# Attention over 32-row blocks in an attention and expert kernel on one core: probabilities turned by VectorE, x of two batches normalised by GpSimd

## What is computed

```python
h = layernorm(x)                                  # no weights
q, k, v = h @ Wq + bq, h @ Wk + bk, h @ Wv + bv
probs = softmax(q @ k.T / sqrt(128))              # per batch, 512 x 512, no mask
x = x + layernorm(probs @ v)
h = layernorm(x)
spikes = sigmoid(h @ W_enc + b_enc)               # 256
cont = spikes @ W_s2c + b_s2c                     # 64
gate = top 2 of softmax(cont @ Wr + br) of 8 experts, made to sum to 1
out = sum_e gate[e] * (relu(cont @ W1[e] + b1[e]) @ W2[e] + b2[e])
dec = sigmoid(out @ W_c2s + b_c2s) @ W_dec + b_dec
x = x + layernorm(layernorm(dec) * ln_g + ln_b)
```

## Time and profile before

| what | value |
|---|---|
| median of 3 runs | 131.04 us (131.02 to 132.98) |
| profiled execution | 130.91 us, its span 129.0 us |
| granted TensorE clock in it, mean | 0.995 |
| TensorE busy | 118.7 us, 92% of the span |
| TensorE weight loads | 80.1 us, beside matmuls |
| VectorE | 94.4 us, 73% |
| ScalarE | 58.8 us, 46% |
| GpSimd | 33.8 us, 26% |
| DMA | 12.42 MB, mean 96 GB/s |

### The profile page before, as it was taken

The page is one execution under the profiler, slowest core; times in us unless marked ns, Lnnn a source line. Parts: engine busy times, 40 slices in busy tenths (PEclk is TensorE's granted clock), DMA queues, the critical chain, the costliest instruction groups (busy, mean ns, idle before and its releaser), DMA issues.

```text
span 129.0 us, 2501 instructions
## 1 busy us (share of the span) xinstructions
PE 118.7 (92%) x815; PEld 80.1 (62%) x815; DVE 94.4 (73%) x400; ACT 58.8 (46%) x173; POOL 33.8 (26%) x70
## 2 busy tenths in 40 slices
PE   6999999999999989999999999999998899998920
PEld 2556786878645767754575994657565455864910
DVE  0858537698989874788957168966889999389672
ACT  1647765556837575204666542053713003903620
POOL 4423503325231162220000132230081043330551
PEclk9999999999999999999999999999999999999998
DMA  3558800000000019700000198000019749720022
GB/s 113 132 121 227 234 18 3 0 0 3 0 5 0 0 50 324 290 8 0 0 0 0 41 293 329 3 0 0 8 48 319 299 138 323 276 86 0 4 79 81
DMA packets 9370, 12.42 MB, mean 96 GB/s; under 512 B 3169, under 2 KB 5998, under 8 KB 9358
## 3 DMA queue, kind: packets, MB, share of 16 engines
q1 hardware_dynamic: 8254, 12.08, 28.5%
q10 hardware_dynamic: 1104, 0.20, 0.8%
HBM read 11.16 MB, written 1.11 MB: 95 GB/s over the span
## 4 chain that ended last, share of the span: by engine, by line
PE 54%; DVE 23%; issue 8%; POOL 7%; ACT 3%; DMA 2%; POOLq 1%; DVEq 0%
PE ps_t L942 10%; POOL rstd L431 7%; PE ps_s L804 6%; PE ps_o L829 6%; PE ps_s L918 5%; PE ps_c L918 4%; DVE stats L1172 3%; PE ps_o L858 3%; PE ps_t L816 3%; DVE x_out L1366 2%; DMA x_in<-in_L_attn_x 2%; DVE xn L1184 2%; PE ps_o L918 2%; PE ps_a L769 2%; DVE neg_max L1200 2%
## 5 line engine op out<-in xcount | busy, mean ns | idle before, releaser
L431 POOL TENSOR_TENSOR rstd<-var_eps,minus_half 128x2 f32<-128x2 f32 (+1 forms) x33 | 25.4, 771 | 88.9 <-DVE var_eps L1177 47.3
L829 PEld LDWEIGHTS ps_o<-v,probsT 128*128 128x128 f32 x128 | 15.6, 191 | 4.6 <-ACT probsT L546 4.1
L829 PE MATMUL ps_o<-v,probsT 128*128 128x128 f32 x128 | 17.5, 279 | 0.4 <-ACT probsT L546 0.3
L942 PE MATMUL ps_t<-gated,w 128*64 128x256 f32 x128 | 17.0, 389 | 0.9 <-DVE gated L1286 0.8
L804 PE MATMUL ps_s<-xnT,yT 128*128 128x512 f32 x32 | 16.0, 596 | 0.1
L541 ACT ACTIVATE probs<-ps_s,neg_max 128x512 f32<-128x512 f32 x16 | 11.0, 687 | 11.1 <-DVE neg_max L1200 11.0
L1200 DVE TENSOR_REDUCE neg_max<-ps_s 128x1 f32<-128x512 f32 x16 | 10.9, 689 | 5.0 <-PE ps_s L804 4.9
L942 PEld LDWEIGHTS ps_t<-gated,w 128*64 128x64 f32 x128 | 8.0, 136 | 8.8 <-DVE gated L1286 4.2
L1286 DVE SCALAR_TENSOR_TENSOR gated<-ps_s,b_minus,gate_all 128x512 f32<-128x512 f32 x14 | 9.9, 744 | 1.9 <-PE ps_s L918 1.9
L546 ACT ACTIVATE probsT<-ps_t 128x512 f32<-128x512 f32 x16 | 9.5, 594 | 2.6 <-PE ps_t L816 2.4
L562 ACT ACTIVATE spikes<-ps_o,bias_half 128x512 f32<-128x512 f32 x6 | 4.1, 687 | 13.5 <-PE ps_o L858 13.4
(11 more groups left out here) (207 smaller groups left out, 218.6 us busy)
## 6 DMA issues: line engine op xcount, KB each, us to landing
gate_all<-gates SPq DMA_DIRECT2D x12, 512.0 KB, 6.0
gate_all<-gates SPq DMA_DIRECT2D x8, 256.0 KB, 3.6
x_in<-in_L_attn_x SPq DMA_DIRECT2D x3, 256.0 KB, 3.6
w<-in_L_ffn_W SPq DMA_DIRECT2D x3, 256.0 KB, 4.4
out<-x_out SPq DMA_DIRECT2D x3, 256.0 KB, 2.0
x_in<-in_L_attn_x SPq DMA_DIRECT2D x2, 128.0 KB, 2.5
out<-x_out SPq DMA_DIRECT2D x2, 128.0 KB, 1.7
w_enc<-in_L_ffn_W_enc SPq DMA_DIRECT2D x1, 128.0 KB, 2.7
```

What stands on the lines that cost most here:

```text
L431: nc.gpsimd.tensor_tensor(rstd[part], var_eps[part], minus_half[:, t0:t1], ALU.pow).then_inc(g_rstd[n], 1)
L829: mm = nc.tensor.matmul(attn_out(t), probsT[:, b % 2, t, k], v[:, b % 2, k], start=(k == 0), stop=(k == T - 1))
L942: mm = nc.tensor.matmul(ps_t[h * M:(h + 1) * M, 0:SH], w2[:, e], gated[:, e, h * SH:(h + 1) * SH], start=False, stop=(e == E - 1))
```

## The change

Batch 0 is done as before. For batches 1 to 3:

- VectorE turns each 128x512 tile of probabilities in 32x32 blocks (`turn_blocks`, one instruction per tile, twelve in all), in place of four TensorE transposes and a ScalarE copy. In `blocks` a partition then holds a key of its 32-key group, and four row groups i of 32 partitions hold four groups of queries.
- `attend(b)` is one step of 64 matmuls: each takes 32 rows (keys), 128 queries as weights and 129 columns of v; the four row groups write to four banks, `ps_o[:, i]`. Column 129 of v is ones, so the product brings the sum of the probabilities, and `exps` doesn't sum any more. For the queries of a row group to be 128 that lie together, `y_out` writes yT in another order of columns.
- Every row group needs all keys' v: v goes to DRAM and returns as v_all, 4 transfers of 32 partitions, 1 MB per batch, on SP's queue ahead of the gates.
- ScalarE copies the product (`att_out`, 128x516), and squares and x_mid read the copy.
- x of batches 2 and 3 is normalised by GpSimd (`x_norm`, L478), and the statistics of x_mid in these two batches are replaced by ScalarE's squares (`mid_square`) against the mean of x, with a small `mid_var` on VectorE.
- Batch 0's last norm goes to ScalarE and GpSimd (`z_norm`, `z_add`), where batch 1's was already. The output is written over x_in, and some other buffers are shared.
- ps_c is gone and ps_o has four banks, in pairs PAIR_X and PAIR_Y; ps_s is PAIR_S. The lists of all engines are written anew; the folding of the biases comes after `attend(1)`, `decode` is one step, and `attend(3)` waits for all eight gate products of batch 0.

The diff, cut to the buffers, the new steps and the parts of the lists of which something is said:

```diff
...
         probs = sb("probs", [P, 2, T, S])
-        probsT = sb("probsT", [P, 2, T, T, P])
+        blocks = sb("blocks", [P, 2, S // 32, T, 32])
+        v_all = sb("v_all", [P, 2, T, T, D + 1])
+        probsT = blocks[:, 0].rearrange("p (t a) b r -> p t a (b r)", t=T)
+        att = sb("att", [P, 2, T, D + 1])
         squares = sb("squares", [P, 2, T, D])
...
+        PAIR_S, PAIR_X, PAIR_Y = ps_s, ps_o[:, 0:2], ps_o[:, 2:4]
...
+        def attn_sums(b, t0, t1):
+            return prob_sum[:, t0:t1] if b == 0 else att[:, b % 2, t0:t1, D]
...
+            sp.wait_ge(g_v_ones, 1)
+            for b in range(1, B):
+                sp.wait_ge(a_v, b + 1)
+                sp.dma_start(v_dram[b].ap(), v[:, b % 2].rearrange("p t d -> p (t d)")).then_inc(d_v_out[b], 16)
+                sp.wait_ge(d_v_out[b], 16)
+                if b == 3:
+                    sp.wait_ge(pe_o, 3)
+                for i in range(T):
+                    sp.dma_start(v_all[32 * i:32 * (i + 1), b % 2].rearrange("a j t d -> a j (t d)"),
+                                 v_dram[b].ap().rearrange("(j a) x -> a j x", j=T)).then_inc(d_v_all[b], 16)
...
+            def x_norm(b):
+                pool.wait_ge(g_rstd[LN_X], parts_done(LN_X, b, 0))
+                if b == 3:
+                    pool.wait_ge(pe_xnT, 3)
+                for t in range(T):
+                    nc.gpsimd.tensor_scalar(xn[:, b % 2, t], x_in[:, b, t], mean_var[:, LN_X, b % 2, t, 0:1],
+                                            rstd[:, LN_X, b % 2, t:t + 1], ALU.subtract, ALU.mult).then_inc(g_xn, 1)
...
+            inverse_std(LN_X, 2, 0)
+            x_norm(2)
             for h in range(2):
                 inverse_std(LN_ATT, 0, h)
                 inverse_std(LN_MID, 0, h)
-            inverse_std(LN_X, 2, 0)
+            inverse_std(LN_X, 3, 0)
+            inverse_std(LN_ATT, 1, 0)
+            x_norm(3)
+            inverse_std(LN_MID, 1, 0)
+            inverse_std(LN_ATT, 1, 1)
+            inverse_std(LN_MID, 1, 1)
...
-                inverse_std(LN_MID, 1, h)
-            inverse_std(LN_X, 3, 0)
+                inverse_std(LN_ATT, 2, h)
+            for h in range(2):
...
             def y_out(b):
                 for i, (bank, s0, s1) in enumerate(y_halves(b)):
                     act.wait_ge(pe_y, b + i + (b > 0) + 1)
-                    nc.scalar.activation(yT[:, b % 2, s0:s1], bank[:, s0:s1], ACT.Identity).then_inc(a_y, 1)
+                    if b == 0:
+                        nc.scalar.activation(yT[:, b % 2, s0:s1], bank[:, s0:s1], ACT.Identity).then_inc(a_y, 1)
+                    else:
+                        nc.scalar.activation(yT[:, b % 2].rearrange("d (t i r) -> d i t r", t=T, i=T),
+                                             bank[:, :].rearrange("d (i t r) -> d i t r", i=T, t=T),
+                                             ACT.Identity).then_inc(a_y, 1)
...
             def exps(b, t):
                 act.wait_ge(v_max, T * b + t + 1)
-                nc.scalar.activation(probs[:, b % 2, t], ps_s[:, t % 2], ACT.Exp, bias=neg_max[:, b % 2, t:t + 1],
-                                     accum_out=prob_sum[:, b % 2, t:t + 1]).then_inc(a_exp, 1)
-            def pT_out(b, t):
-                act.wait_ge(pe_pT, T * b + t + 1)
...
+            def att_out(b):
+                act.wait_ge(pe_o, b + 2)
+                if b == 3:
+                    act.wait_ge(v_mid, 2 * T)
+                nc.scalar.activation(att[:, b % 2], ps_o[:, :, 0:D + 1], ACT.Identity).then_inc(a_att, 1)
             def attn_squares(b, h):
-                act.wait_ge(pe_o, 2 * b + h + 1)
+                if b == 0:
+                    act.wait_ge(pe_o, h + 1)
+                else:
+                    act.wait_ge(a_att, b)
                 for t in range(TH * h, TH * (h + 1)):
-                    nc.scalar.activation(squares[:, b % 2, t], attn_out(t), ACT.Square,
+                    nc.scalar.activation(squares[:, b % 2, t], attn_out(b, t), ACT.Square,
                                          accum_out=square_sum[:, b % 2, t:t + 1]).then_inc(a_square, 1)
+            def mid_square(b, h):
+                act.wait_ge(v_mid, T * b + TH * (h + 1))
+                for t in range(TH * h, TH * (h + 1)):
+                    nc.scalar.activation(squares[:, b % 2, t], x_mid[:, b, t], ACT.Square, scale=-1.0,
+                                         bias=mean_var[:, LN_X, b % 2, t, 0:1],
+                                         accum_out=mid_square_sum[:, b % 2, t:t + 1]).then_inc(a_mid_square, 1)
             def hT_out(b):
...
+            def attend(b):
+                pe.wait_ge(v_blocks, T * b)
+                pe.wait_ge(d_v_all[b], 16 * T)
+                if b == 1:
+                    pe.wait_ge(v_mid, T)
+                    pe.wait_ge(a_square, T)
+                elif b == 2:
+                    pe.wait_ge(a_att, 1)
+                    pe.wait_ge(v_b2, 1)
+                    pe.wait_ge(v_bdec, 1)
+                    pe.wait_ge(v_bcont, 1)
+                    pe.wait_ge(v_logit, 1)
+                else:
+                    pe.wait_ge(v_gated, E)
+                for j in range(S // 32):
+                    for i in range(T):
+                        rows = slice(32 * i, 32 * (i + 1))
+                        mm = nc.tensor.matmul(ps_o[:, i, 0:D + 1], blocks[rows, b % 2, j].rearrange("p t r -> p (t r)"),
+                                              v_all[rows, b % 2, j % T, j // T],
+                                              start=(j == 0), stop=(j == S // 32 - 1))
+                mm.then_inc(pe_o, 1)
...
-                attend(m, 3)
...
-                    to_spikes(b)
-                    route(n)
+            project_y(3)
+            project_v(3)
+            attend(2)
+            scores(3, 0)
+            scores(3, 1)
+            turn_h(1)
+            encode(1, 0)
+            encode(1, 1)
+            hidden_pair(0, 0)
+            to_cont(1)
+            scores(3, 2)
+            route(1)
+            expert_biases(0)
+            hidden_pair(0, 1)
+            scores(3, 3)
+            for e in range(4):
+                expert_out(0, e)
+            turn_h(2)
+            hidden_pair(0, 2)
+            hidden_pair(0, 3)
+            encode(2, 0)
+            encode(2, 1)
+            for e in range(4, E):
+                expert_out(0, e)
+            attend(3)
+            to_cont(2)
+            to_spikes(0)
...
+            def mid_var(b, h):
+                part = slice(TH * h, TH * (h + 1))
+                dve.wait_ge(a_mid_square, T * (b - 2) + TH * (h + 1))
+                nc.vector.tensor_scalar(var_eps[:, LN_MID, b % 2, part], mid_square_sum[:, b % 2, part], 1.0 / D, EPS,
+                                        ALU.mult, ALU.add).then_inc(v_veps[LN_MID], 1)
...
+            def turn_blocks(b, t):
+                dve.wait_ge(a_exp, T * b + t + 1)
+                if b >= 2:
+                    dve.wait_ge(pe_o, b)
+                nc.vector.transpose(blocks[:, b % 2, :, t], probs[:, b % 2, t]).then_inc(v_blocks, 1)
...
+            row_max(3, 0)
+            attn_var(2, 0)
+            row_max(3, 1)
+            mid_add(2, 0)
+            attn_var(2, 1)
+            turn_blocks(3, 0)
+            mid_add(2, 1)
+            turn_blocks(3, 1)
+            mid_var(2, 0)
+            router_top(1)
+            row_max(3, 2)
+            gate_hidden(0, 0)
+            mid_norm(2, 0)
+            mid_var(2, 1)
+            gate_hidden(0, 1)
+            router_index(1)
+            row_max(3, 3)
+            turn_blocks(3, 2)
+            gate_hidden(0, 2)
+            mid_norm(2, 1)
+            gate_hidden(0, 3)
+            turn_blocks(3, 3)
+            router_gates(1)
+            for e in range(4, E):
+                gate_hidden(0, e)
...
             attn_var(3, 0)
-            mid_stats(3, 0)
+            mid_add(3, 0)
...
```

More of the change, by code:

```diff
@@ L259, in attention_moe_block @@
         d_ln = sem("d_ln")
+        d_v_out = [sem(f"d_v_out{b}") for b in range(B)]
+        d_v_all = [sem(f"d_v_all{b}") for b in range(B)]
         d_gateT = [sem(f"d_gateT{i}") for i in range(2)]
@@ L1027, in _ @@
             scores(0, 3)
-            turn_probs(0, 2)
-            attend(0, 1)
-            pe.wait_ge(g_s2c, 1)
-            for h in range(2):
-                for c in range(HC):
-                    mm = nc.tensor.matmul(ps_c[h * M:(h + 1) * M, 1, 0:1], w_s2c[:, c], ones[:, 0:1],
-                                          start=(c == 0), stop=(c == HC - 1))
-            mm.then_inc(pe_bcont, 1)
+            turn_probs(2)
+            attend_first(1)
             project_v(1)
             scores(1, 0)
-            turn_probs(0, 3)
@@ L1039, in _ @@
-            attend(0, 2)
+            turn_probs(3)
+            attend_first(2)
             scores(1, 1)
-            turn_probs(1, 0)
-            attend(0, 3)
+            attend_first(3)
             scores(1, 2)
-            turn_probs(1, 1)
-            attend(1, 0)
```

(32 more changed lines are left out.)

671 lines of the change are left out of this document (312 added, 359 removed).

## The result

| | before | changed |
|---|---|---|
| median | 131.04 us | 151.03 us (150.49 to 153.85, 5 runs) |
| ratio | | 1.151, 95% interval 1.148 to 1.154 |
| profiled execution | 130.91 us, span 129.0 | 153.40 us, span 151.6 |
| granted TensorE clock, mean | 0.995 | 0.915 |

The forecast was 131.3 us, with a range to 137.5. The changed kernel is 20 us slower. Its profiled execution is one of the longer ones; those near the median had spans of 148.7 to 149.2 us and a mean clock of 0.927 to 0.933.

What follows compares the result with a forecast made beforehand. TensorE was taken as the bound, VectorE close behind. Its 5.3 us saved go into new queue waits; the last gate product at 117.0 against 116.2 and +0.4 in all give span 129.4, plus 1.9: 131.3 us, range 127.0 to 137.5.

Steps and rivals of the forecast that it cites:

- (a): Start to attend(1): VectorE has 10.5 us of work and about 1.3 of waits; attend(1) runs 31.4 to 34.9 us.
- (b): attend(1) to attend(2): one queue-ordered chain of 12.5 us where TensorE has 9.1 of work; attend(2) 47.5 to 51.0 us.
- (c): After attend(2): new TensorE wait of 3.6 us before encode(1) at 56.8; gate product (0,7) ends at 74.2 us.
- (d): attend(3) waits for gate product (0,7), runs 75 to 78.5 us; VectorE waits 4.2 us until its squares at 80.0.
- (e): From 80.0 us to the last gate product: VectorE has 34.6 us of work, 2.4 us added; it ends at 117.0.
- VectorE's sum: VectorE's work over the whole span: gains and losses net to nothing, 94.4 us stays about 94.
- the block transpose: VectorE's twelve turns of 128x512 probabilities: 0.73 us each, 8.8 in all; bounds 0.69 and 1.25 each.
- v_all: v's return from DRAM: lands within 9 us of its copy, costs nothing, hidden behind scores and norms.
- the clock: TensorE's clock: its 3.6 us idle in (c) could bring it down, but nothing was counted for it.
- R5: Slower rival: small waits in (a) to (e) sum up, GpSimd's norms, late v_all and clock included: 133.8 to 136; chance 0.11.
- Four row groups together: TensorE's attention products in batches 1 to 3: four row groups overlap, 3.5 us per batch; upper bound 7.0 in pairs.
- GpSimd's norm: Normalising x of batches 2 and 3 on GpSimd: 0.6 us per tile, 2.4 for four, up to twice 0.54 each.

Runs made afterwards that it cites:

- the best order: The changed kernel with nine queue changes and three more moves on VectorE, no instruction less: 130.79 us, ratio 0.998 to the kernel before.
- the kernel with three steps moved: The changed kernel with ScalarE's hT copy of batch 1 and VectorE's b_cont moved earlier, GpSimd's batch 1 z_add behind decode(2)'s inverse root: 144.28 us.

## Why the prediction was wrong

Its walk beside the profile after, start or end of each in us:

| step | forecast | measured | of the difference, new in this step |
|---|---|---|---|
| (a) attend(1) ends | 34.9 | 36.1 | 1.2 |
| (b) attend(2) ends | 51.0 | 56.0 | 3.8, of it 3.1 of clock |
| (c) encode(1) starts | 56.8 | 61.8 | 0 |
| (c) route(1) ends | 61.9 | 70.3 | 3.4, of it 2.9 of clock |
| (c) gate product (0,7) ends | 74.2 | 84.4 | 1.8, of it 1.7 of clock |
| (d) attend(3) ends | 78.5 | 90.1 | 1.4 |
| (e) last gate product ends | 117.0 | 137.6 | 9.0, of it 1.7 of clock |
| end of the span | 129.4 | 151.6 | 1.6 |

So of the 22.2 us that this profile lies above the forecast, 9.4 are of clock and 12.8 are not, 7.3 of these in (e).

**Right:** the new wait in (c). The chain of waits of the changed kernel is the one that the prediction summed (start, length, what):

```profile
57.14 0.70 DVE neg_max L1258
...
57.87 0.69 ACT probs L596
...
59.41 0.61 DVE neg_max L1258
...
60.04 0.69 ACT probs L596
60.73 0.58 ACT squares L617 x4
61.31 0.49 ACT hT L630
```

It gave 3.6 us of TensorE's waiting, and 3.44 was measured. The queue move that took hT forward was one of the three that brought 6.7 us together. Right too were VectorE's sum, the block transpose (0.70 for 0.73), and v_all: of TensorE's waits none named that transfer, which landed 3.1 to 5.8 us after issue.

**Wrong, first, the clock.** The prediction counted nothing for it, on the ground that from 123.5 to 127.5 us no matmul ran and the clock stayed full. A quiet stretch behind the last matmul was no evidence for short waits between matmuls: in the profile after, waits of 1.7 to 3.4 us were followed by 3.3 to 7 us at half clock. In it 9.5 us were lost so; filling four waits brought 3.5 of time. It was put in R5 as one small thing among others, and should have been a rival of its own, since (c) forecast just such a wait.

**Wrong, second, and the largest of the steps, (e).** It took VectorE for the bound behind attend(3), gave it 34.6 us of work, and so had 38.5 us to the last gate product. VectorE's sum was right, with 33.8 us. But TensorE was busy from there until the expert sum behind the last gate product for 43.28 of 48.7 us, 1.7 of it lost at half clock:

```profile
90.10:138.80 48.70, 43.28 (x319) 26.59 (x319) 33.81 (x130) 17.93 (x65) 11.84 (x19) 0.96 0.39 135
```

The kernel before had said so. Its last attention ends at 76.6 us, in TensorE's timeline

```profile
75.47 1.12 PE L829 MATMUL ps_o<-v,probsT 128*128 128x128 f32 x8
```

and from there it needs 39.6 us to its last gate product, with TensorE busy for 38.1 of them. In the changed kernel the same distance is 47.5 us, with 40.8 of TensorE's work at full clock, 1.7 lost at half clock and 5.0 of waits. The change leaves more of the experts to do behind attend(3) (decode(0), `to_spikes`(0)) than it took ahead. So the work alone is 2.3 us more than the 38.5 forecast; the best order needs 42.0 us here. Each stage must be checked against the sum of every engine, not only of the one that the change loads. The larger part is the waits for gate products, 1.85, 1.24 and 1.54 us among them, which the prediction didn't look for: scaled weights, norms and router gates now stood ahead of gate products. Moving them, and two gate products of (c), brought 4.9 us by the medians.

**Smaller.** The terms that the prediction lists for (b) add up to 14.4 us, and it went on with 12.5. With 14.4 its own sum would have given 133.2 us, which is still in its range and far from 151. The run took 14.3 us from attend(1) to attend(2), 1.2 of them of clock, so 13.1 at full clock: that 12.5 came closer than the listed terms is luck. The last 1.6 us came behind the last gate product: batch 1's `z_add` stood on GpSimd ahead of the inverse root of decode(2). From the last gate product to the end of the span it took 14.0 us, where 12.4 were forecast; with `z_add` moved behind that root, in the kernel with three steps moved, 12.9.

**Sizes.** Four row groups together: I took 3.5 us, 3.8 was measured. The Trainium skill (TensorE: Matmul & The Clock Gate, Part 3, Measured speedup vs the span model) has 3.07 for four tiles of 32 rows with 512 columns, from which I had estimated 4.6 us; the runs show 3.5 times, so the measured 3.8 us lie between the two estimates. GpSimd's norm took 0.81 us where I took 0.6. The Trainium skill (GPSIMD Engine Reference, 8. Key points) has VectorE about twice as fast; the rows show 0.81 against 0.342, 2.4 times. It cost nothing (150.91 us without it); the wait behind it stayed because ScalarE's queue held the next step longer. TensorE's work fell by 3.1 to 3.6 us and not 5.3; three attentions of 3.8 in place of 3.5 are 0.9 of that, and the rest is not accounted for.

**Why the best order only draws level:** 3.6 us less work than before, but 2.9 us more waits and 0.6 more at the end. The attention in one step of 64 products needs a whole batch's turned probabilities and its v at once, and gives up the tile by tile mixture that kept TensorE fed before. That last sentence is argued from the traces, not tried.

## What to carry to other kernels

When work is taken off the busiest engine and the queues are rewritten, price the queues, not the instructions: here the same instructions took 151.0 or 130.8 us. For each stage add up every engine's work, and for each copy that the busiest engine waits for, list what stands ahead of it on its own engine. Where TensorE gets waits between matmuls like those here (1.1 to 3.4 us), count half clock behind them as a case of its own, since the same wait was followed by it in one profile and not in another.
